# Second mixture of a two-layer model: tokens sorted by expert on the chip, blocks of 128 sorted rows through their own expert

## What the kernel computes

```python
logits = flat @ router_w                                   # [1024, 64]
scores = softmax(logits)
_, topk_idx = top_k(logits + router_bias, 4)               # 4 of 64 experts per token
topk_scores = take_along_axis(scores, topk_idx); topk_scores /= topk_scores.sum(-1)
comb = zeros([1024, 64]).at[arange(n)[:, None], topk_idx].set(topk_scores)
g = silu(einsum('nd,edf->nef', flat, wg))                  # wg, wu: [64, 256, 64]
u = einsum('nd,edf->nef', flat, wu)
routed = einsum('ne,nef,efd->nd', comb, g * u, wd)         # wd: [64, 64, 256]
shared = einsum('nsh,shd->nd', silu(flat @ swg) * (flat @ swu), swd)   # 2 shared experts, 256 hidden each
mixture = routed + shared
```

## Time and profile before

| what | value |
|---|---|
| three runs | 1287.93, 1288.07, 1289.17 us; median 1288.07 us |
| the profiled execution | 1286.95 us, with a span of 1285.2 us from first to last instruction |
| mean granted TensorE clock | 0.935 of full speed |
| busy share | PE 88%, DVE 71%, ACT 54%, POOL 34% |
| projections of layer 1 | about 760 to 815 us |
| recurrence | about 815 to 903 us |
| output block of the linear attention | about 904 to 950 us |
| RMS norm and MLP | about 950 to 1013 us |
| `mixture1` | 1013 to 1285 us |

### The profile page before, as it was taken

How to read it: one execution, slowest core, us unless ns; L and a number is a source line. 1 busy time by engine, 2 the same in 40 slices (tenths; PEclk the granted TensorE clock), 3 DMA queues, 4 the chain that set the end, 5 groups by cost and what they waited for, 6 DMA issues and landing times. The chain is left out here.

```text
span 1285.2 us, 20632 instructions
## 1 busy us (share of the span) xinstructions
PE 1127.8 (88%) x6922; PEld 638.0 (50%) x6922; DVE 917.3 (71%) x1500; ACT 691.5 (54%) x1217; POOL 439.1 (34%) x253
## 2 busy tenths in 40 slices
PE   6866988999999899999997879756779999999997
PEld 4455855555555555555553754422344544444443
DVE  4978159999999899999995154799634155655554
ACT  3554267888777787777884124500554044344443
POOL 2821054444444354444220004254420033333331
PEclk9965988999999999999998987898879999999999
DMA  5243018887777787777779010400000344444331
GB/s 157 78 132 113 1 33 138 143 143 142 138 140 141 132 144 144 144 141 140 133 137 213 2 41 1 125 1 0 1 1 1 78 112 118 114 121 122 117 118 49
DMA packets 332820, 126.79 MB, mean 99 GB/s; under 512 B 273296, under 2 KB 328064, under 8 KB 332736
## 3 DMA queue, kind: packets, MB, share of 16 engines
q1 hardware_dynamic: 332736, 125.72, 45.6%
HBM read 57.26 MB, written 1.31 MB: 46 GB/s over the span
## 5 line engine op out<-in xcount | busy, mean ns | idle before, releaser
L1067 DVE SCALAR_TENSOR_TENSOR a_pr<-a_ex,a_rtot,a_pr 128x1024 f16<-128x1024 f32 x128 | 206.4, 1613 | 3.7 <-ACT a_pr L992 3.6
L848 POOL TENSOR_TENSOR a_rnorm<-a_ss,a_power 128x8 f32<-128x8 f32 x32 | 80.2, 2508 | 258.4 <-DVE a_ss L1033 258.3
L2058 POOL TENSOR_TENSOR e_sg<-e_sg,e_cb 128x512 f32<-128x512 f32 x64 | 82.0, 1282 | 242.1 <-ACT e_sg L2006 242.1
L1054 DVE TENSOR_REDUCE a_nmax<-psum 128x1 f32<-128x1024 f32 x128 | 155.4, 1214 | 12.9 <-PE psum L907 9.2
L984 ACT ACTIVATE a_ex<-psum,a_nmax 128x1024 f32<-128x1024 f32 x128 | 142.8, 1116 | 12.4 <-DVE a_nmax L1054 8.9
L992 ACT ACTIVATE a_pr<-a_ex,a_rtot 128x1024 f16<-128x1024 f32 x128 | 147.4, 1152 | 0.0
L889 PE MATMUL psum<-a_wh,xT_h 128*128 128x128 f16 (+1 forms) x512 | 115.3, 248 | 3.8 <-PEq L578 1.2
L2014 ACT ACTIVATE e_hh<-e_hf 128x512 f16<-128x512 f32 x64 | 40.3, 630 | 143.4 <-DVE e_hf L2083 143.4
L890 PE MATMUL psum<-a_wl,xT_h 128*128 128x128 f16 (+1 forms) x512 | 115.1, 248 | 0.0
L891 PE MATMUL psum<-a_wh,xT_l 128*128 128x128 f16 (+1 forms) x512 | 115.1, 248 | 0.0
L921 PE MATMUL psum<-a_pT,a_vh 128*128 128x512 f16 x256 | 98.2, 384 | 7.6 <-DMA a_pT<-a_pr 7.6
(11 more groups left out here) (349 smaller groups left out, 2706.8 us busy)
## 6 DMA issues: line engine op xcount, KB each, us to landing
e_cb<-comb_by_expert SPq DMA_DIRECT2D x64, 256.0 KB, 3.8
wf<-in_L_ffn_W_gate SPq DMA_DIRECT2D x32, 128.0 KB, 2.4
wf<-in_L_ffn_W_up SPq DMA_DIRECT2D x32, 128.0 KB, 2.4
wf<-in_L_ffn_W_down SPq DMA_DIRECT2D x32, 128.0 KB, 2.8
e_guf<-in_L_ffn_wg SPq DMA_DIRECT2D x32, 128.0 KB, 2.3
e_guf<-in_L_ffn_wu SPq DMA_DIRECT2D x32, 128.0 KB, 2.3
e_dnf<-in_L_ffn_wd SPq DMA_DIRECT2D x32, 128.0 KB, 2.1
a_wf<-in_L_attn_wq SPq DMA_DIRECT2D x16, 128.0 KB, 3.0
```

The source lines that it names most:

```text
L1054: dve.tensor_reduce(nmax[:, k:k + 1], score_banks(m), AX.X, ALU.max, negate=True).then_inc(max_ready, 1)
L1067: dve.scalar_tensor_tensor(pr[k][:, 1, :], ex[e][:, :], rtot[:, e:e + 1], pr[k][:, 0, :], ALU.mult, ALU.subtract).then_inc(p_ready, 1)
```

## The change

- In the projections, `Router1` ranks the assignments instead of making `comb`: PE counts with matmuls by a matrix of ones and one of an upper triangle (`make_places`), and DVE finds for each token its four places in the list sorted by expert (`find_slots`), and a table of windows (`find_windows`): for each of 64 experts the offset of its first 128 rows, and 32 extra windows for the further rows of experts with more than 128. Three small DMAs write this table and one reads it back into one partition. POOL also makes row-major high and low parts of the tokens.
- In the recurrence, POOL issues two indirect DMAs ahead of each step's multiplication, 32 in all: each scatters 128 token rows of 1 KB to their sorted places in DRAM (`sorted_tokens`). When all have landed, SP issues 32 DMA transposes of 128 rows by 512 halfwords each, which bring the sorted list back as columns (`xTs`).
- A new block `Windows1` runs 48 steps of two windows: 16 steps of extra windows, whose expert number comes from the table, then 32 steps of main windows. It runs all 48 whatever the counts are. POOL copies the two windows out of `xTs` at offsets read from the table, PE makes 24 gate and up matmuls and 12 down matmuls of 128 columns, ACT copies each window's output into `yT` at the offset (which it also reads from the table), and later windows overwrite the rows beyond an expert's own.
- Then PE turns the 32 tiles of `yT`, ACT and DVE take them out of PSUM in turn, and SP stores them to DRAM (`sorted_outputs`, 4 MB in eight DMAs).
- The shared experts' down projection moves into the output block (8 times 12 matmuls of 256 columns, after each tile of the projection), and the MLP's weights are loaded and split there. POOL gathers the sorted outputs back by token with 32 indirect DMAs, 8 in the output block and 24 in the MLP block, and DVE adds them by weight with 32 instructions (`take`) between the MLP's steps.
- The final silu, multiplication, addition and store run in the MLP block. `mixture1` is gone.

The ranking, on PE and DVE in the projections' block (`find_windows` follows in the same way with some twenty small instructions on at most 32 partitions):

```diff
+    def make_places(self, pe):
+
+        pe.wait_ge(self.masks_done, 2)
+        pe.wait_ge(self.sel_ready, 1)
         for n in range(NT):
+            for i in range(n):
+                pe.matmul(self.pos[:, n, :], self.ones16[:, :], self.sel16[:, i, :], start=(i == 0), stop=False)
+            pe.matmul(self.pos[:, n, :], self.upper16[:, :], self.sel16[:, n, :], start=(n == 0), stop=True)
+        for n in range(NT):
+            last = pe.matmul(self.count, self.ones16[:, :], self.sel16[:, n, :], start=(n == 0), stop=(n == NT - 1))
...
+    def find_slots(self, dve):
...
+        chain(dve.tensor_tensor_scan(upto, self.ones[:, :], self.count, 0.0, ALU.mult, ALU.add))
+        chain(dve.scalar_tensor_tensor(start1, upto, 1.0, self.count, ALU.add, ALU.subtract))
+        chain(dve.tensor_tensor(key, self.pos, bcast(start1, 1, NT), ALU.add))
+        chain(dve.tensor_tensor(key, key, self.sel[:, :, :], ALU.mult))
+        for n in range(NT):
+            chain(dve.max(self.best_key[:, n, :], self.key[:, n, :]))
```

In the recurrence's block, on SP and POOL:

```diff
                     shared.load(sp)
-                    router.wait_stored(sp)
+                    router.store_table(sp)
+                    sp.wait_ge(xs_stored, 16 * NT * K1)
+                    for block_at in range(0, SLOTS1, P):
+                        sp.dma_start_transpose(xTs[:, :, block_at:block_at + P], xs[block_at:block_at + P, :]).then_inc(xs_loaded, 16)
...
                     for s in range(STEPS):
+                        for i in range(2 * s, 2 * s + 2):
+                            n, k = i // K1, i % K1
+                            pool.indirect_dma_start(xs, bass.IndirectOffsetOnAxis(ap=router.slot[:, n, k:k + 1], axis=0),
+                                                    xhl[:, n, :], None).then_inc(xs_stored, 16)
                         pool.wait_ge(st_ready, s + 1)
```

`Windows1`, in order: SP's loads, POOL's copies, ACT's outputs and step:

```diff
+                def load(s, b, extra):
+                    if not (fixed(s) and s < 2):
+                        sp.wait_ge(self.gul_ready, s - 1)
+                    if extra:
+                        at = [sp.value_load(table[0:1, bass.ds(2 * s + WINDOWS + e, 1)], min_val=0, max_val=E1 - 1) for e in range(2)]
+                        for j, src in enumerate((self.wg, self.wu)):
+                            for e in range(2):
+                                sp.dma_start(gu_f[b][:, j, e, :, :].rearrange("p c f -> p (c f)"),
+                                             src[bass.ds(at[e], 1), :, :].rearrange("e (p c) f -> p (e c f)", p=P))\
+                                  .then_inc(self.gu_loaded[b], 16)
...
+                    if not (fixed(s) and s < 2):
+                        sp.wait_ge(self.dnl_ready, s - 1)
...
+                def step(s, b):
+                    if not (fixed(s) and s < 2):
+                        pool.wait_ge(self.gu_ready, s - 1)
+                    for e in range(2):
+                        off = pool.value_load(table[0:1, bass.ds(2 * s + e, 1)], min_val=0, max_val=SLOTS1)
+                        pool.tensor_copy(xw[b][:, e, :, :], xTs[:, :, bass.ds(off, P)]).then_inc(self.x_ready, 1)
...
+                def outputs(s, b):
+                    act.wait_ge(self.y_ready, s + 1)
+                    for e in range(2):
+                        off = act.value_load(table[0:1, bass.ds(2 * s + e, 1)], min_val=0, max_val=SLOTS1)
+                        if not (fixed(s) and s == 0 and e == 0):
+                            act.wait_ge(self.y_done, 2 * s + e)
+                        act.activation(yT[:, :, bass.ds(off, P)],
+                                       psum[:, 2 + 2 * e + b, 0:D].rearrange("p (c t) -> p c t", c=DC), ACT.Copy,
+                                       scale=1.0 / WSCALE).then_inc(self.y_done, 1)
...
+                    act.activation(sg[b][:, :], psum[:, b, 0:P], ACT.Silu, scale=1.0 / WSCALE).then_inc(self.silu_ready, 1)
+                    if gate_up is not None:
+                        gate_up_high(s + 2, b, gate_up)
+                    if not (fixed(s) and s == 0):
+                        outputs(s - 1, 1 - b)
+                    if down is not None:
+                        down_high(s + 1, 1 - b, down)
```

In the MLP's block, on DVE, after each step from the fifth on:

```diff
+                    def take(i):
+
+                        for j in range(4 * i, 4 * i + 4):
+                            n, k = j % NT, j // NT
+                            dve.wait_ge(gathered[k], 16 * NT)
+                            if k:
+                                dve.wait_ge(mixed, j - NT + 1)
+                            dve.scalar_tensor_tensor(mix[:, n, :], yg[:, n, k, :], share[:, n, k:k + 1], mix[:, n, :],
+                                                     ALU.mult, ALU.add).then_inc(mixed, 1)
```

More of the change, by code:

```diff
@@ L1185, in load @@
+        self.extra, self.extra_upto, self.extra_before, self.mine, self.part = (
+            tmp(n, [OVER, E1]) for n in ("extra", "extra_upto", "extra_before", "mine", "part"))
+        self.found = tmp("found", [OVER, 2])
     def load(self, sp):
@@ L1326, in low, with down @@
         pool.tensor_tensor(self.h_l[k][:, :], self.hf[k % 2][:, :], self.h_h[k][:, :], ALU.subtract).then_inc(self.hl_ready, 1)
-def gated_linear_attention(nc, env, w):
+    def down(self, pe, n):
+        pe.wait_ge(self.hl_ready, 2 * self.QUARTERS)
+        if n >= 4:
+            pe.wait_ge(self.y_done, n - 3)
+        half, cols = n // 4, slice((n % 4) * P, (n % 4 + 1) * P)
+        out = self.psum[:, 4 + n % 4, 0:D]
+        for q in range(self.QUARTERS):
+            hh, hl = self.h_h[2 * q + half][:, cols], self.h_l[2 * q + half][:, cols]
+            wh, wl = (x[q][:, :, :].rearrange("p c d -> p (c d)") for x in (self.dn_h, self.dn_l))
+            pe.matmul(out, hh, wh, start=(q == 0), stop=False)
+            pe.matmul(out, hl, wh, start=False, stop=False)
+            last = pe.matmul(out, hh, wl, start=False, stop=(q == self.QUARTERS - 1))
+        last.then_inc(self.y_ready, 1)
@@ L1681, in _ @@
                     dve.tensor_tensor(o[:, :, :], o[:, :, :], silu_g[:, :, :], ALU.mult).then_inc(og_ready, 1)
+                    router.share_out(dve, chain, equal[:, :, :], share)
+                    for i, (whole, high, low) in enumerate(mlp_parts):
+                        dve.wait_ge(mlp_high, i + 1)
+                        dve.scalar_tensor_tensor(low, whole, WSCALE, high, ALU.mult, ALU.subtract)
                     for n in range(NT):
@@ L1687, in _ @@
                 def _(pool):
+                    windows.wait_stored(pool)
+                    gather(pool, 0)
                     shared.hidden(pool, 0)
@@ L1711, in _ @@
                         shared.high(act, k - 1)
+                    for i, (whole, high, low) in enumerate(mlp_parts):
+                        act.wait_ge(mlp_loaded[i], 16)
+                        act.activation(high, whole, ACT.Copy, scale=WSCALE).then_inc(mlp_high, 1)
                     for n in range(NT):
@@ L1722, in _ @@
                         square(act, s1, 1, n)
+                        shared.down_done(act, n, mix)
                 @block.tensor
@@ L1751, in _ @@
                         last.then_inc(y_ready, 1)
-        with ExitStack() as local:
+                        if n:
+                            shared.down(pe, n - 1)
+                    shared.down(pe, NT - 1)
+            norm.close()
             def tmp(name, shape, dt=F32):
```

784 lines of the change are left out of this document (437 added, 347 removed).

## The result

The changed kernel takes 1327.1 us (median of 4 runs, 1324.95 to 1328.0) and the kernel before 1288.0 us (1287.82 to 1289.17): a ratio of 1.030, 95% interval 1.028 to 1.031. It is slower by 3.0%, where 1.0% faster was forecast; the range ended at 1325.

What follows compares the result with a forecast made beforehand. PE's columns were taken to bound `mixture1` and DVE the recurrence. Without `mixture1`, 1013.3 us plus 8, 0, 34, 6.5, 160, 15.5, 21, 9.7 and 4.5 made 1272.5, with 1.75 outside the span 1274; forecast 1275 us, range 1232 to 1325.

Steps and rivals of the forecast that it cites:

- projections: Block before the recurrence: DVE's added instructions in `find_slots` and `find_windows` count in full, +8 us.
- recurrence: Two scatters a step at 1.1 us fit POOL's idle time, 4.55 of 4.57 us, so +0 us.
- way back: After the recurrence: SP waits for all scatters, then 32 transposes at 1.2 us each, partly hidden, +34 us.
- windows, with fill: `Windows1`: loads bound the steps; fill 6.5 us, 32 main steps 94 us, 16 extra steps 66 us.
- turn: After the windows: 32 tiles at 0.41 us, 13 us, and 2.4 for the block's change, +15.5 us with the store.
- output block: High parts of MLP weights 4.2 us, gathers 2 us, PE's wait 4.8 us, 96 matmuls 10.3 us: +21 us.
- MLP: MLP block: four `take` make DVE's step 3.97 us, longer than PE's 2.59; seven steps at 1.38, +9.7 us.
- tail: After PE's last matmul: addition, product, addition, hand-overs and a store of 2.6 us, +4.5 us.
- slower by POOL: Rival, chance 0.10: an indirect DMA of 2.0 us makes recurrence steps 6.35 us, +28 us, total 1325 us.
- value loads: Rival, chance 0.19: ACT and SP stand in value loads in the windows; at 1.0 us each, total 1307 us.
- the prediction's own rule: Windows: value loads cost 40 us per us up to 0.6 us each, 64 above that.
- The rival's 3.85 us a step: Clock rival, chance 0.09: at 1.2 GHz PE takes 3.85 us a window step, above 2.95: +29, total 1304 us.

Runs made afterwards that it cites:

- e1: Changed kernel with POOL's 32 scatters replaced by 32 plain stores of the same bytes from SP's queue, tokens left unsorted: 1266.75 us (ratio 0.983).
- e2: Changed kernel with 14 of the 32 scatters issued in the block before the recurrence, the other 18 spread over its steps: 1320.4 us (ratio 1.024).
- e4: Changed kernel with SP issuing each window step's gate and up load ahead of the previous step's down load: 1325.8 us (ratio 1.028).
- e5: Changed kernel with fixed expert numbers in place of SP's value loads in the extra window steps: 1310.1 us (ratio 1.018).
- e9: Changed kernel with skewed loads in all window steps and fixed expert numbers in place of SP's value loads: 1284.9 us (ratio 0.999).
- e3: Changed kernel with 16 transposes of 256 rows in place of 32 of 128 rows: 1308.7 us (ratio 1.016).
- e7: Changed kernel with PE multiplying only the high halves in the windows, 12 of 36 matmuls a step: 1322.4 us (ratio 1.027).
- e8: Changed kernel with 10 scatters issued early, 256-row transposes, and loads skewed in main steps alone: 1278.7 us (ratio 0.9925).

## Why the prediction was wrong, step by step

The sum was made for 1274.25; the profiled execution took 1326.98. Both start from the 1013.3 us of the old kernel, and each term can be measured from the same marks. The table's "by" is measured less forecast; they add up to 52.6 of 52.7 us.

| term | forecast | measured | by |
|---|---|---|---|
| projections (first product of the recurrence, 817.00 to 830.11) | 8 | 13.1 | +5.1 |
| recurrence (first product to POOL's last, 82.4 to 104.4) | 0 | 22.0 | +22.0 |
| way back (934.5 to 977, less the old end, 4.1) | 34 | 38.4 | +4.4 |
| windows, with fill (977 to 1162.5) | 166.5 | 185.5 | +19.0 |
| turn | 15.5 | 19.5 | +4.0 |
| output block | 21 | 22.7 | +1.7 |
| MLP | 9.7 | 5.6 | -4.1 |
| tail | 4.5 | 5.0 | +0.5 |

The forecast lay 13 us below the kernel before, so the 22 us of the recurrence were enough by themselves to turn its sign; with the 19 us of the windows they carried the time out of the range.

**Recurrence: the step that failed.** The prediction has "Then POOL needs 2.2 + 2.35 = 4.55 us of 4.57: just hidden." Alone a scatter takes 0.96 us, so the price was right where POOL has the time to itself. But I gave all 32 one price, left out the gaps between POOL's instructions, and left POOL 0.02 us a step in which to be wrong. With the gaps even the last step, whose scatters met no scan, took 4.81 us from product to product (927.34 to 932.15), not 4.55. The first of each pair is held until DVE's scan is over: 3.05 us (runs e1, e2). In the earlier trace rows POOL's wait of 2.23 us is for that very scan; a new instruction put in it runs beside the scan, and I had not asked what that does to either. The reading behind it was wrong too: "bound by DVE, busy 79.4 of 88 us" counts 11 scans at 3.43 us that take 2.29 with no product beside them. What bound the step was product and scan in turn, and POOL's idle time was no free time. The rival "slower by POOL" had the path, POOL's own stream, though not the reason, at a mean price of 2.0 us; measured is 1.7, and 22 us for its 28. Its chance of 0.10 was too low for a step with no slack.
The Trainium skill, "SBUF — State Buffer", section "SBUF: two separate sides", in the box on "DVE blocks DMA", says that GpSimd can't write a DMA's descriptors while VectorE holds the port pair they share, in its two-port modes; in the next section, that a DMA of some 620 ns takes some 3100 beside a VectorE copy. The trace agrees in kind: 0.96 alone, 3.05 beside a scan, and an end 0.82 us after the scan's. That page of the Trainium skill, in "Who interferes with whom", names copies, casts and tensor_scalar as such operations and not the scan; here the scan does it.

**Windows: the loop was right, two of its terms too small.** 32 main steps were put at 2.95 us and took 3.12 (5 us in all); 16 extra ones at 4.1 and took 4.75 (10 us); fill and end had the rest. In the main steps the forecast's reason, the load held behind the down half in SP's order, is shown by e4: without it 2.46 us. In the extra ones the named bound was wrong: "SP's own work there is 3.7 us and fits" counted six issues and 0.9 for two value loads. They are 3.05 with the gaps between them and 1.53, together 4.58, and SP is the bound (e4, e5, e9). A value load takes some 0.65 us on every engine, against 0.45 taken. What differs is what hides it: on SP nothing does, while on ACT the second one runs beneath the first output's 0.38 us and leaves a gap of 0.34, as the prediction's term for it had said. By the prediction's own rule (40 us per us up to 0.6, then 64) the 0.65 gives some 9 of these 15 us. So the rival "value loads" had a real share; it was to decide from 0.71 on, and the price stayed just below.
The Trainium skill's floor of about 600 ns for loading a register ("DMA: Bandwidth & Descriptors", "Latency and other measured facts"), which the prediction quoted, is near the 0.65 us of a whole value load; the load instruction in it is recorded with 0.27.

**Way back: right in kind.** Expected was 1.2 us each, by the share of the data path; measured 1.31, by SP's issue. That is a different reason, and it mattered: a bound by issue can be halved by larger instructions (e3), one by data can't. At 512 rows the data path gives 238 GB/s. That is near the 261 GB/s of the Trainium skill ("DMA: Bandwidth & Descriptors", "Latency and other measured facts"), which the prediction set against the 97 of the rows. Why attention's transposes, from SBUF, stand at 97 was not tried.

**Projections.** Of the 13.1 us, 2.5 are not of this block. Layer 1's first turn on PE starts at 764.45 us, against 761.96 in the kernel before; the code of layer 0 ahead of it is the same, and in the traces of the twelve experiments it starts anywhere from 762.6 to 765.3 us. The other 10.6 stand against 8. All DVE work was counted in full, 8 us. Not counted was that the gate's additions stand behind `find_slots` on DVE while PE's gate matmuls wait for them. DVE's timeline of that stretch:

```profile
796.41 4.64 DVE L1272 CAST g_r_sel<-g_r_sel 128x512 f16<-128x512 f32 x1
...
817.09 0.42 DVE L1951 TENSOR_TENSOR g_silu_g<-psum,g_bg 128x256 f32<-128x256 f32 x1 [1.83 <-PE psum L1885]
```

PE's own row there, and two stretches of it (columns as in the earlier trace rows):

```profile
814.97 8.10 PE L1885 MATMUL psum<-g_wg,g_xT 128*128 128x256 f32 x24 [4.60 <-DVE g_silu_g L1951]
```

```profile
815.00:820.50 5.50, 5.50 (x13) 4.38 (x14) 1.10 (x4) 0.00 (x0) 0.00 (x0) 0.51 0.00 0
820.50:823.20 2.70, 2.57 (x12) 1.90 (x11) 1.37 (x4) 0.00 (x0) 0.00 (x0) 1.00 0.00 0
```

PE waits 4.6 us and then, at a granted clock of 0.51 (the lower level, 1.2 GHz), gives a tile every 1.7 us, twice the 0.86 of before, and DVE waits for it; from 820.5 us on the clock is 1.00 and the tiles come at 0.86 again. Three tiles at 0.85 us more come to the 2.6 us by which 10.6 exceeds 8. The cast took 4.64 us where 0.69 was counted. It began 0.24 us after POOL's subtraction of 4.13 us (796.17) and ended 0.75 us after it: the scatter's stall, the other way round. It cost nothing here: behind the cast DVE is idle for 5.83 us, waiting for ACT, and PE's counting matmuls, which read the cast's result, come at 807.11, behind the value projection.

**Turn, output block, MLP, tail.** The turn's tiles took 0.58 us, not 0.41: PE was busy 17.5 of the 19.5 us there, at a granted clock of 0.58, which I had not applied to it. The output block came within 2 us. In the MLP a step with four `take` is 3.57 us, not 3.97. The 0.70 us that DVE idles in a step, waiting for ACT, is still there (1283.50 to 1284.20); what was smaller is the four `take`, 1.67 us in place of 1.88, and each long instruction begins some 0.08 us before the one ahead of it is over.

**The clock.** It did fall to 0.50 and 0.58, as the rival had it, but with a third of PE's work left no step of the windows changed (e7). The rival's 3.85 us a step at 1.2 GHz counted the 36 matmuls one behind the other. In pairs they kept PE busy for some 2.1 us of a main step (71.51 of 107.5 us), and for 2.4 of an extra one.

## What to carry to other kernels

An instruction that is to fill an engine's idle time has to be priced beside the one it will run with, not alone. Ask first what that idle time waits for: here it was the very instruction that shut the engine out. And where a sum says "just hidden", the chance belongs to the rival. Before calling a queue's time free, add up its stream, waits apart: issues, value loads and gaps; here that alone was the bound of 16 steps. Ask of each transfer stretch whether issue or data sets its pace, since they have different cures.

## What the runs showed of the hardware

- A float32 scan of 128x1024 on DVE and a product of the same size on POOL did not run side by side: the scan is recorded with 2.29 us alone and 3.43 (kernel before) or 4.21 (e2) when begun beside a product, and ended some 2.15 us after the product's end in both.
- An indirect DMA on POOL (128 rows of 1 KB) takes 0.96 us to issue, 1.27 with the gap to the next (e2), and 2.81 to 3.06 when it begins under such a scan.
- A value load from the table takes some 0.65 us of SP, ACT or POOL, of which 0.27 to 0.29 are the load.
- A transposing DMA from DRAM holds SP for 1.27 us at 128 rows of 512 halves, 1.31 at 256 rows and 2.2 at 512; landing 2.7, 3.9 and 4.7 us.
- With the same matmuls, the main steps had a granted clock of 0.60 at 3.12 us a step and of 0.87 at 2.49 (e8): of the two levels, 1.2 and 2.4 GHz, mostly the lower, then mostly the upper. Rows of 1067 to 1155 us in the changed kernel and of 1060 to 1100 us in e8:

```profile
1067.00:1155.00 88.00, 59.44 (x1012) 47.38 (x1008) 57.59 (x139) 50.41 (x140) 41.17 (x56) 0.60 0.43 125
```

```profile
1060.00:1100.00 40.00, 25.72 (x576) 20.21 (x576) 33.69 (x80) 29.67 (x80) 23.13 (x32) 0.87 0.54 157
```
